# Hybrid layer on one core: second-pass attention masks move from TensorE to GpSimd, and VectorE and ScalarE are reordered inside the sessions

## The reference, cut to what matters

```python
kqv = x @ Wqkv + bqkv                      # x: (4, 1024, 512), 16 heads of 32
scores = einsum('bsnh,btnh->bnst', k, q) / sqrt(32)
scores = triu(scores) + -10000.0 * tril(ones, k=-1)
attn = softmax(scores, axis=2)             # over the keys s; query t sees s <= t
out = einsum('bnkq,bknh->bqnh', attn, v) @ Wo + bo
```

## Time and profile before

| | us |
|---|---|
| median of 3 runs | 3169.89 (3167.56 to 3171.26) |
| the profiled execution's own time | 3168.84 |
| its span | 3167.1 |
| TensorE busy (matmuls) | 2895.3 (91%) |
| VectorE busy | 1943.5 (61%) |
| ScalarE busy | 1181.2 (37%) |
| GpSimd busy | 696.5 (22%) |

### The profile page before, as it was taken

The page is one execution under the profiler, slowest core; times in us unless marked ns, Lnnn a source line. Parts: engine busy times, 40 slices in busy tenths (PEclk is TensorE's granted clock), DMA queues, the critical chain, the costliest instruction groups (busy, mean ns, idle before and its releaser), DMA issues.

```text
span 3167.1 us, 58505 instructions
## 1 busy us (share of the span) xinstructions
PE 2895.3 (91%) x20788; PEld 2064.0 (65%) x20788; DVE 1943.5 (61%) x2910; ACT 1181.2 (37%) x1877; POOL 696.5 (22%) x997
## 2 busy tenths in 40 slices
PE   3888989999898899999988889999989889999998
PEld 3655477777665457777765545777776544777776
DVE  2545465777745555677765556377776444647777
ACT  2244334444124423444323441444422443244442
POOL 3300012333210001333311001133322000023331
PEclk7999999999999999999999999999999999999999
DMA  9322011111232202111133220211123230111112
GB/s 342 84 60 65 18 52 49 46 50 47 82 73 59 58 14 54 46 48 49 41 94 74 48 48 14 67 49 48 38 68 88 48 78 18 42 50 51 46 45 77
DMA packets 163781, 192.03 MB, mean 61 GB/s; under 512 B 43963, under 2 KB 103995, under 8 KB 161787
## 3 DMA queue, kind: packets, MB, share of 16 engines
q1 hardware_dynamic: 156126, 175.57, 20.5%
q10 hardware_dynamic: 7456, 13.90, 1.4%
HBM read 106.99 MB, written 23.36 MB: 41 GB/s over the span
## 4 chain that ended last, share of the span: by engine, by line
PE 69%; DVE 13%; issue 8%; ACT 4%; SPq 3%; DMA 3%; POOL 1%; ACTq 1%; DVEq 0%; POOLq 0%
PE ps L745 14%; PE ps L746 13%; PE ps L747 13%; DVE mneg L1648 5%; PE ps L1110 4%; PE ps L993 3%; PE ps L923 3%; PE ps L866 3%; PE ps L1096 2%; PE ps L908 2%; PE ps L1119 2%; PE ps L1156 2%; PE ps L861 2%; ACT PR L1298 1%; DMA win_raw<-in_t 1%
## 5 line engine op out<-in xcount | busy, mean ns | idle before, releaser
L745 PE MATMUL ps<-uh,win 128*128 128x512 f32 x1536 | 625.4, 407 | 18.1 <-POOL win L1893 17.4
L746 PE MATMUL ps<-ul,win 128*128 128x512 f32 x1536 | 603.3, 393 | 0.0
L747 PE MATMUL ps<-uh,win 128*128 128x512 f32 x1536 | 602.0, 392 | 0.0
L1648 DVE TENSOR_REDUCE mneg<-ps 128x1 f32<-128x896 f32 (+7 forms) x512 | 366.9, 752 | 274.6 <-PE ps L866 273.1
L1298 ACT ACTIVATE PR<-ps 128x1024 f32<-128x1024 f32 (+3 forms) x384 | 293.3, 808 | 334.0 <-PE ps L908 307.2
L745 PEld LDWEIGHTS ps<-uh,win 128*128 128x128 f32 x1536 | 289.8, 189 | 92.8 <-POOL win L1893 19.8
L747 PEld LDWEIGHTS ps<-uh,win 128*128 128x128 f32 x1536 | 289.8, 189 | 64.9
L746 PEld LDWEIGHTS ps<-ul,win 128*128 128x128 f32 x1536 | 290.6, 189 | 53.8
L1762 DVE TENSOR_TENSOR LM<-ps,LM 128x512 f32<-128x512 f32 x256 | 170.2, 686 | 242.4 <-PE ps L1110 198.4
L1973 POOL TENSOR_SCALAR_AFFINE_SELECT LM<-LM 128x512 f32<-128x512 f32 x256 | 209.5, 830 | 491.4 <-ACT LM L1401 491.4
L923 PE MATMUL ps<-PR,V 128*32 128x512 f32 (+3 forms) x1536 | 285.9, 497 | 3.6 <-ACT PR L1298 2.3
(11 more groups left out here) (220 smaller groups left out, 5039.8 us busy)
## 6 DMA issues: line engine op xcount, KB each, us to landing
raw<-in_t SPq DMA_DIRECT2D x128, 256.0 KB, 2.8
QS<-EV SPq DMA_DIRECT2D x192, 128.0 KB, 2.5
KS<-EV SPq DMA_DIRECT2D x168, 128.0 KB, 2.6
in_t<-tiles ACTq DMA_DIRECT2D x10, 1024.0 KB, 9.2
XN<-in_L_attn_a_x_dram SPq DMA_DIRECT2D x40, 256.0 KB, 5.1
win_raw<-in_L_attn_a_Wqkv_dram SPq DMA_DIRECT2D x34, 256.0 KB, 3.4
win_raw<-in_t SPq DMA_DIRECT2D x32, 256.0 KB, 2.7
edec<-ed_t SPq DMA_DIRECT2D x512, 16.0 KB, 1.6
```

Of the source, the lines that this page charges most:

```text
L745: pe.matmul(dst, hi_l, hi_r, start=first, stop=False)
L746: pe.matmul(dst, hi_l, lo_r, start=False, stop=False)
L747: return pe.matmul(dst, lo_l, hi_r, start=False, stop=last)
L1648: dve.tensor_reduce(mneg[:, hh, t:t + 1], flat[:, off:off + (t + 1) * P], AX.X, ALU.max, negate=True).then_inc(a_max.sem, 1)
```

## The change

For the eight units with a diagonal block the two mask matmuls are gone, and the scores are written directly. Instead GpSimd zeroes the masked triangle of the exponentials with one `affine_select` per unit on [128, 2, 128] elements (`clear`); `weigh` of such a unit waits for GpSimd (`cleared`) and no longer for ScalarE. GpSimd's order is new: the residual stands ahead of the first `group_lo`, and the clears stand between scalings and `group_lo`. On VectorE `project_lo` moves behind the maxima of group 2k+1. On ScalarE the exponentials 0 and 1 of the next pair move ahead of `take` of c = 1. On TensorE the units 2 and 3 are issued one after the other, each with its own wait, where both waits stood ahead of both before.

```diff
+DIAGONAL = [u for u, (c, k) in enumerate(ORDER) if k >= 4 * c]      # 0,1,2,3,5,6,7,8
@@ TensorE, scores_b
                         ex.wait(pe, p, max(u - 1, 0))
-                        if s * P >= c * HB:
-                            for hh in range(2):
-                                pe.matmul(ps[:, score_bank(u) + hh, 0:P], identb[:, :], mask_st[:, :], start=True, stop=False, skip_group_check=True)
...
-                                          QS[:, home(pair, hh), t0:t0 + n], start=s * P < c * HB, stop=True, skip_group_check=True)
+                                          QS[:, home(pair, hh), t0:t0 + n], start=True, stop=True)
@@ TensorE, weigh
-                    ex.wait(pe, p, u + 1)
+                    if u in DIAGONAL:
+                        cleared.wait(pe, p, DIAGONAL.index(u) + 1)
+                    else:
+                        ex.wait(pe, p, u + 1)
@@ TensorE, sessions
-                            scores_b(p, pair, (2 * k + 2, 2 * k + 3))
+                            if k == 0:
+                                scores_b(p, pair, (2,))
+                                scores_b(p, pair, (3,))
+                            else:
+                                scores_b(p, pair, (2 * k + 2, 2 * k + 3))
@@ ScalarE, after the sessions
-                        take(p, g, hf, 1)
                         if ahead:
                             for u in range(2):
                                 exponentials(p + 1, u)
+                        take(p, g, hf, 1)
@@ VectorE, inside the loop over the session's groups before, behind it now
-                                    if g < GROUPS - 1 and k < 4:
-                                        project_lo(g + 1, k, False)
+                            if hf == 0 and g < GROUPS - 1 and k < 4:
+                                project_lo(g + 1, k, False)
@@ GpSimd
+                def clear(p, units):
+                    for u in units:
+                        until(ex, p, u + 1)
+                        v = PR[:, u % 4, :, 0:P]
+                        pool.affine_select(out=v, in_=v, compare_op=ALU.is_ge, fill=0.0, base=0,
+                                           pattern=[[0, 2], [1, P]], channel_multiplier=-1).then_inc(cleared.sem, 1)
+                residual()
                 group_lo(b * 4 + 1)
                 until(qkw_lo, b * 4 + 1, 1)
-                residual()
                 for g in range(GROUPS):
+                    p = b * 8 + g * 2
+                    clear(p, DIAGONAL[:4])
+                    if g > 0:
+                        scale(g - 1, 0)
+                    clear(p, DIAGONAL[4:])
+                    if g > 0:
+                        scale(g - 1, 1)
+                    clear(p + 1, DIAGONAL[:4])
                     if g < GROUPS - 2:
                         group_lo(b * 4 + g + 2)
                         until(qkw_lo, b * 4 + g + 2, 1)
-                    for c in range(2):
...
+                    clear(p + 1, DIAGONAL[4:])
+                for c in range(2):
+                    scale(GROUPS - 1, c)
```

More of the change, by code:

```diff
@@ L290, in hybrid_layer @@
         ex = signal("ex", 12)
+        cleared = signal("cleared", 8)
         pv = signal("pv", 12)
@@ L373, in hybrid_layer @@
                        bt_act, cm_act, ed_act, ds_act, dt_act, seg_act],
-            "gpsimd": [wv_lo, qkw_lo, xzw_lo, ln_rstd, *o_scaled, cp_pool, xd_pool, xp_pool, sel_pool, st_pool],
+            "gpsimd": [cleared, wv_lo, qkw_lo, xzw_lo, ln_rstd, *o_scaled, cp_pool, xd_pool, xp_pool, sel_pool, st_pool],
             "tensor": [ln_tp, v_pe, w_pe, pj, a_pe, m_pe, st_pe, pv, z_pe, t_pe, u_pe, al_pe, dc_pe,
@@ L1927, in residual, with scale @@
                     pool.sem_inc(s_tick, 1)
+                def clear(p, units):
[5 more added lines that the diff above has]
+                residual()
                 group_lo(b * 4 + 1)
                 until(qkw_lo, b * 4 + 1, 1)
-                residual()
-                for g in range(GROUPS):
+                def scale(g, c):
+                    until(o_rec, b * 4 + g, c + 1)
+                    part = OT[:, g, c * HB:(c + 1) * HB]
+                    pool.tensor_tensor(part, part, den[:, c, :], ALU.mult).then_inc(o_scaled[c].sem, 1)
+                    until(o_scaled[c], b * 4 + g, 1)
+                for g in range(GROUPS):
+                    p = b * 8 + g * 2
[6 more added lines that the diff above has]
+                    clear(p + 1, DIAGONAL[:4])
                     if g < GROUPS - 2:
```

## The result

The changed kernel takes 3119.51 us (median of 4 runs, 3117.19 to 3126.79) against 3168.72 for the kernel before in the same comparison. The ratio is 0.9848, with a 95% interval of 0.983 to 0.9867: 49 us faster, or 42 to 54. The profiled execution took 3117.19 with a span of 3115.5.

A forecast was written before the change was run, and what follows sets the result against it. TensorE, busiest, was held in attention sessions mainly by its wait on VectorE's maxima, which stood behind project_lo. 37.0 + 4.9 + 17.9 - 8 - 4 = 47.8 us off 3168.84 gave 3121, range 3106 to 3146.

The forecast's parts named there:

- The low part behind the maxima: Projecting sessions: with project_lo after the maxima, group 2k+1 to the next takes 2.24, not 3.01; 48 x 0.77 = 37.0 us gained.
- The masks in sessions: Sessions 1 to 3 of 12 projecting pairs: removed mask matmuls save 4.9 us; elsewhere TensorE's idle time hides them.
- the starts of pairs: Start of each pair: no masks, units 2 and 3 apart, exponentials ahead of take; 17.9 us gained.
- The clears: GpSimd's affine_select on 2 x 128 columns: some 0.4 us each, bounds 0.29 and 1.43, mostly hidden.
- the long ones: Rival: GpSimd clears of 1.43 us each give 3137, chance 0.08; 1.43 occurred only beside one certain VectorE instruction.
- cost beside `group_lo`: Pairs with hf = 1 and g < 2: clears behind group_lo delay TensorE's unit 5; 8 us lost, bounds 7 and 16.
- The residual: Moved into the layer norm, it meets four or five VectorE L1478 instructions; 4 us lost, bounds 0 and 18.
- The stacked rows: Rival: DMAs stacking rows for pair 2g+2 land late, 12 pair starts lose 1 us each; 3133, chance 0.10.
- nothing else moves: Rest of the kernel: no further change; scalings keep their place behind the inversions they wait for.
- The wait on the maxima: TensorE waiting for VectorE's maxima in the attention sessions: sign of being right, a fall from 83.7 to about 45 us.
- GpSimd's pace: Rival: GpSimd's clears become the path beyond about 2.7 us each; at 3.5 us, 3269; chance 0.04.
- The clock: Rival: TensorE in the sessions loses the 48 us if 30 stretches at 1.2 GHz were added; chance 0.02.

The follow-up runs named there:

- e1: The kernel before with one edit alone, VectorE's project_lo behind the maxima of group 2k+1: 3123.57 us, ratio 0.9858.
- e2: The changed kernel with only the move of VectorE's project_lo behind the maxima undone: 3157.53 us, ratio 0.9972.
- e4: The changed kernel with GpSimd's clear of unit 5 ahead of group_lo in pairs with hf = 1: 3105.88 us, ratio 0.9798.
- e9: e5 with 120 semaphore increments at the start of TensorE's stream, shifting its later code: 3110.04 us, ratio 0.9809.
- e7: e4 with the 512 mask matmuls put back on TensorE beside the clears: 3118.58 us, ratio 0.9853.
- e6: e4 with ScalarE's take of c = 1 ahead of exponentials 0 and 1 again: 3112.94 us, ratio 0.9822.
- e11: e5 with units 2 and 3 issued together again, behind the wait for the exponential of unit 1: 3107.2 us, ratio 0.9803.
- e5: e4 with the residual back behind the first group_lo, as in the kernel before: 3106.47 us, ratio 0.9811.
- e3: The changed kernel with the 512 mask matmuls back on TensorE and no clears on GpSimd, all reordering kept: 3117.93 us, ratio 0.9845.
- e8: e4 with each clear over all columns of its unit instead of the diagonal block alone: 3104.56 us, ratio 0.9795.
- e10: e5 with 60 semaphore increments at the start of TensorE's stream, shifting its later code: 3096.17 us, ratio 0.9765.

## Why the prediction was right, point by point

*The low part behind the maxima, 37.0 forecast.* Shown by e1 (39.6 by the pairs) and e2 (39.7 by the pairs, 38 by the median). The chain is 2.19, not 2.24. The low part's margin against the next maxima, put at 0.1 to 0.15, is 0.24 in the row shown. The forecast that nothing is late next holds.

*The masks in sessions, 4.9, and the starts of pairs, 17.9.* Together 22.8. The pairs without a late row or a wait for the clear, set against those of e1, are shorter by 1.05, 1.53 and 1.54 in the projecting ones, by 0.5 in 1-2, 3-4 and 5-6 and by 0.2 in 6-7 (the lengths of e4, and of e9 for 1-2 and 6-7): 5.8 per batch, 23 in all. Taken out one by one, the parts give some 16 (masks, e7), 7 (ScalarE's order, e6) and 3 (units 2 and 3 apart, e11), which is a little more than together. The start of a projecting pair was forecast at 2.5 to the projection and is 2.57.

*The clears.* One takes 0.41 (I took 0.4). All 256 of them (minimum, median, maximum in ns):

```profile
L1942 POOL TENSOR_SCALAR_AFFINE_SELECT PR<-PR x256: 406/406/422, 144.1 to 2621.3; 128x256 f32<-128x256 f32 x128
```

The prediction set the long ones aside as met beside one certain VectorE instruction; in the kernel before 56 of the 68 above 1 us ran beside that one (L1588) and 12 beside others. Their cost beside `group_lo` was forecast at 8 us and is 11.4 in TensorE's waits: this term was mis-sized. I had `group_lo`, 0.1 of handing over and the clear; the handing over behind `group_lo` is 0.33, from the weighing to the next group it is 0.36 where I had 0.25, and the distance between groups grew by 1.41, not 1.0.

*The residual, 4 forecast.* L1486 did meet it, three times per batch and not four or five (0.89, 0.86 and 1.60 in place of 0.54), and TensorE's second wait for the layer norm's transposes grew from 0.40 to 0.76; the first, 0.99, is as long in e5. Timeline of VectorE, TensorE and GpSimd in the layer norm of batch 1:

```profile
854.98 0.89 DVE L1486 TENSOR_SCALAR xh<-XN,mv,rstd 128x512 f32<-128x512 f32 x1
...
856.43 0.86 DVE L1486 TENSOR_SCALAR xh<-XN,mv,rstd 128x512 f32<-128x512 f32 x1
...
860.88 1.60 DVE L1486 TENSOR_SCALAR xh<-XN,mv,rstd 128x512 f32<-128x512 f32 x1
...
854.52 0.65 PE L759 MATMUL ps<-ident,xh 128*128 128x128 f32 x4 [0.99 <-DVE xh L1486]
855.93 0.66 PE L759 MATMUL ps<-ident,xh 128*128 128x128 f32 x4 [0.76 <-DVE xh L1486]
...
852.88 10.74 POOL L1932 TENSOR_TENSOR X<-XN,bob 128x512 f32<-128x512 f32 x8 [0.34 <-POOL KS L1923]
```

In batches at the full clock e5 gives back 0.6, in three batches, 1.8 us: the mechanism is right and its direct size was too large, since a VectorE instruction that arrives late in a GpSimd one waits only for its rest. With the slow stretches that follow the longer waits it is 4.4 on average (e5), near the forecast 4, but by luck: the prediction had not thought of the clock here.

*The stacked rows.* The rival said that they come late; they did not. Another transfer on the same engines did, the maxima's row, which the prediction left out, for 5.2 us. That nothing else moves is the one wrong step, and a small one.

*The wait on the maxima*, forecast at 45, is 55.0. It is 44.5 with the low part alone, and 46.6 in e3 and in e7, which have the masks and all reordering: some 8 of the 10 us between are mask matmuls that turned into idle time, as the prediction argued for sessions without projections, though it did not carry this into the number.

Sum with the measured sizes: 39.6 + 23 - 11.4 - 5.2 and the residual's 1.8 to 4.4 make 42 to 44, at the lower end of the measured 42 to 54. The forecast's 47.8 came nearer to the median partly by luck: the gains were 3 larger than forecast, and the losses beside `group_lo` and of the late row 3.4 and 5.2 larger. GpSimd's pace is refuted by e8 for clears of 0.73 on average. The clock: TensorE was at the full 2.4 GHz in the sessions of the window below (length, busy us by engine, granted clock, DMA share, GB/s). In batches 2 and 3 the sessions contain one stretch of 3.4 us at 1.2 GHz each, as those of batches 1 and 3 do in the kernel before, so this rival did not come true there.

```profile
886.00:1084.00 198.00, 176.02 (x1248) 104.56 (x1246) 110.92 (x153) 87.06 (x127) 35.01 (x63) 1.00 0.27 62
```

The best kernel of the series is e10 (3096), whose shift has no explained gain; of the edits with an explained one, e4 (3106): the change with one clear ahead of `group_lo`.

## What to carry to other kernels

Where two engines alternate (matmul group, reduction, matmul group), ask of every instruction between the two whether the next round needs it; moving one that it does not need gave 40 us, while taking 512 matmuls off the busiest engine gave 13 net, and less once its replacement stood behind a long instruction. When work moves to another engine, its place in that engine's order matters more than its duration: making the clears 1.8 times as long cost nothing, one of them behind a 2.4 us instruction, eight times, cost 11 us. Price each part of a compound change alone, by lengths of one repeated stretch, which repeat to 0.06 us where nothing disturbs them, while the medians scatter by 5; and follow an added wait to the clock, which can cost more than the wait.

## What the runs showed of the hardware that was not expected

With a 16 KB packet on the instruction queue, 1.1 us long on average, the other queue moved 0.33 MB in place of 0.59 in the 3 us behind the row's issue, and the DMA of 8 KB, which otherwise lands 2.0 to 2.5 us after its issue (by its semaphore), took 3.2 to 3.9. Such packets come every 180 to 310 instructions of TensorE in the sessions, with a median of 258 over the execution, and moving that code by 60 or 120 instructions moved the late landings to other pairs. Not every packet does it: behind pair 2 in e9 it held up nothing. Removing matmuls thus moved the waits of a DMA that has nothing to do with them.

Two waits of TensorE for the layer norm, 1.2 and 0.76 us long, came before 3.4 us at 1.2 GHz, and the batch's stretch took 50.17 in place of 47.58 (e4); the same with 0.99 and 0.75 left the clock at 2.4 GHz.
